# Reordering the tail of a two-layer transformer kernel: output merges, cluster logits and dense tiles on TensorE, copies and roots on ScalarE

## What is computed

```python
x = L0_attn_x
x = _layernorm(x + _L0_attn_ref(x, ...))   # 128 heads, latent projections
x = _layernorm(x + _L0_ffn_ref(x, ...))    # gated FFN with low-rank terms
x = _layernorm(x + _L1_attn_ref(x, ...))   # 32 heads, 8 key heads, causal
x = _layernorm(x + _L1_ffn_ref(x, ...))
```

```python
dots = jax.nn.softmax(x @ centroids.T / TEMPERATURE, axis=-1)   # 64 clusters
hits = dots > THRESHOLD
query_sel = jnp.any(hits, axis=1)        # one value a row
cluster_sel = jnp.any(hits, axis=0)      # one value a cluster, over all rows
row_sel = cluster_sel[assignments]       # one value an output column
dense = x @ weight.T + bias
out = jnp.where(query_sel[:, None] & row_sel[None, :], dense, 0)
```

## Time and profile before

| what | value |
|---|---|
| median of 3 runs | 2517.71 us (2509.7 to 2518.99) |
| the profiled execution | 2519.56 us, of which 2517.5 us are the span of the trace |
| PE busy in the span | 2465.6 us (98%) |
| DVE, ACT, POOL busy | 1555.6, 1396.0, 1152.8 us |
| granted TensorE clock, mean | 0.99 of full speed |
| first merge of the last key head starts | 2437.96 us into the span |

### The profile page before, as it was taken

The page is one execution under the profiler, slowest core; times in us unless marked ns, Lnnn a source line. Parts: engine busy times, 40 slices in busy tenths (PEclk is TensorE's granted clock), DMA queues, the critical chain, the costliest instruction groups (busy, mean ns, idle before and its releaser), DMA issues. The chain is left out here.

```text
span 2517.5 us, 40557 instructions
## 1 busy us (share of the span) xinstructions
PE 2465.6 (98%) x12632; PEld 1858.7 (74%) x12632; DVE 1555.6 (62%) x2796; ACT 1396.0 (55%) x2171; POOL 1152.8 (46%) x1155
## 2 busy tenths in 40 slices
PE   7999999999999999999998999899999999999998
PEld 4777777777777777777775588778888888888875
DVE  6666666666666666666664523276657557566576
ACT  3677777777777777777776433233424324234241
POOL 1556555555555555656564243234334234343331
PEclk9999999999999999999999999989999999999999
DMA  6122222222222222222221422121000010010100
GB/s 215 43 47 53 45 53 50 48 53 45 53 45 56 48 55 45 53 45 53 45 55 39 131 88 85 39 84 42 10 32 17 25 42 17 25 42 2 36 1 34
DMA packets 47613, 125.40 MB, mean 50 GB/s; under 512 B 6034, under 2 KB 23442, under 8 KB 41427
## 3 DMA queue, kind: packets, MB, share of 16 engines
q1 hardware_dynamic: 47570, 124.85, 18.5%
HBM read 80.27 MB, written 10.49 MB: 36 GB/s over the span
## 5 line engine op out<-in xcount | busy, mean ns | idle before, releaser
L427 DVE TENSOR_REDUCE row_max<-ps_max 128x1 f32<-128x512 f32 x1024 | 670.9, 688 | 193.0 <-PE ps_max L517 170.6
L292 POOL TENSOR_TENSOR p_parts<-probs,p_parts 128x1024 f16<-128x1024 f32 x256 | 547.5, 2149 | 367.0 <-ACT p_parts L346 366.0
L341 ACT ACTIVATE probs<-ps_score 128x1024 f32<-128x1024 f32 x512 | 523.1, 1022 | 241.8 <-PE ps_score L533 221.1
L531 PE MATMUL ps_score<-Q,K 128*128 128x512 f32 x1024 | 408.0, 398 | 2.2 <-ACT probs L341 2.1
L533 PE MATMUL ps_score<-Q,K 97*128 97x512 f32 x1024 | 407.1, 398 | 0.0
L517 PE MATMUL ps_max<-KX,Q 68*128 68x512 f32 x1024 | 378.8, 411 | 3.8 <-DVE row_max L427 3.6
L421 DVE TENSOR_TENSOR Q<-ps_x,Q 64x512 fp32r<-64x512 f32 x254 | 175.0, 689 | 241.9 <-ACT Q L336 238.2
L346 ACT ACTIVATE p_parts<-probs 128x1024 f16<-128x1024 f32 x256 | 269.5, 1053 | 4.0
L517 PEld LDWEIGHTS ps_max<-KX,Q 68*128 68x128 f32 x1024 | 189.3, 190 | 76.4 <-issue 28.1
L531 PEld LDWEIGHTS ps_score<-Q,K 128*128 128x128 f32 x1024 | 194.5, 190 | 60.4 <-ACT probs L341 12.0
L533 PEld LDWEIGHTS ps_score<-Q,K 97*128 97x128 f32 x1024 | 195.5, 191 | 39.3
(11 more groups left out here) (292 smaller groups left out, 4399.8 us busy)
## 6 DMA issues: line engine op xcount, KB each, us to landing
Q<-Q SPq DMA_DIRECT2D x64, 512.0 KB, 4.3
ffn_raw<-in_w_ffn SPq DMA_DIRECT2D x22, 768.0 KB, 4.4
w_raw<-in_w_qrope SPq DMA_DIRECT2D x32, 512.0 KB, 3.7
wq_raw<-in_wq SPq DMA_DIRECT2D x8, 1024.0 KB, 5.5
wo_raw<-in_wo SPq DMA_DIRECT2D x8, 1024.0 KB, 4.8
content_k<-probs SPq DMA_DIRECT2D x8, 512.0 KB, 6.8
Q<-content_q SPq DMA_DIRECT2D x64, 64.0 KB
K<-content_k SPq DMA_DIRECT2D x64, 64.0 KB
```

What stands on the lines that cost most here:

```text
L292: pool.tensor_tensor(p_lo[:, j, :, :], probs[:, j, 0:PAIRED, :], p_hi[:, j, :, :], ALU.subtract)\
L341: act.activation(probs[:, j, 2 * half:2 * half + 2, :], ps_score[half][:, :, :], ACT.Exp, scale=SCALE).then_inc(exped, 1)
L427: dve.tensor_reduce(row_max[:, t, j:j + 1], ps_max[t % 2][:, :], axis=AXX, op=ALU.max)\
L531: pe.matmul(ps_score[half][:, k, :], K1[:, b, t * P:(t + 1) * P], Q1[:, b, j, :], start=True, stop=False)
```

## The change

On PE the last merge moves in front of the first logits, with the transposes of tiles 6 and 7 behind these. Dense tile 0 now starts before the first logits are transposed, and the second logits, their transposes, the cluster count and the column's product stand two dense tiles earlier than before. On ACT each copy `high_x(t - 2)` stands in front of `root(t)`, and the copy of the first logits stands behind the load of the Exp table. DVE, POOL and SP keep their order. No instruction does other work than before; only the places at which dense tiles are cut differ.

```diff
--- before.py
+++ after.py
@@ -1577,11 +1577,10 @@
             take_outputs(KV, NU - 1)
             root(1, x_base)
             for t in range(2, TT):
+                high_x(t - 2)
                 root(t, x_base)
-                high_x(t - 2)
-                if t == TT - 2:
-                    take_logits(0)
             act.activation(unused[:, :], eps[:, :], ACT.Exp)
+            take_logits(0)
             high_x(TT - 2)
             high_x(TT - 1)
             exp_soft(0)
@@ -1961,37 +1960,34 @@
             merge(True, tk, 1)
             outputs(LAST, NU - 1)
             merge(True, tk, 2)
-            for t in range(TT - 3):
+            for t in range(ST + 1):
                 turn_x(t)
+                merge(True, tk, t + 3)
                 if t == 0:
-                    merge(True, tk, 3)
                     pe.wait_ge(o_low, ONE + LAST + 1)
-                    continue
-                if t == ST:
-                    pe.wait_ge(cl_ready, 1)
-                    logits(0)
-                merge(True, tk, t + 3)
-            turn_x(TT - 3)
+            turn_x(ST + 1)
+            pe.wait_ge(cl_ready, 1)
+            logits(0)
+            turn_x(TT - 2)
+            turn_x(TT - 1)
+            pe.wait_ge(cl_ready, 3)
+            dense_tile(0, 0, 6)
             turn_logits(0)
-            turn_x(TT - 2)
-            pe.wait_ge(cl_ready, 3)
-            dense_tile(0)
-            turn_x(TT - 1)
-            dense_tile(1)
+            dense_tile(0, 6)
             logits(1)
-            dense_tile(2, 0, 6)
+            dense_tile(1, 0, 4)
             turn_logits(1)
-            dense_tile(2, 6)
-            dense_tile(3)
+            dense_tile(1, 4)
+            dense_tile(2, 0, 4)
             for b in range(NB):
                 pe.wait_ge(hits, b + 1)
                 last = pe.matmul(ps_c[0:NCL, 0:1], any_hit[:, b, :], ones[:, 0:1], start=b == 0, stop=b == NB - 1)
             last.then_inc(hits_counted, 1)
-            dense_tile(4, 0, 6)
+            dense_tile(2, 4, 9)
             pe.wait_ge(onehot_made, 1)
             pe.matmul(ps_h[:, :], ones[0:NCL, :], onehot, start=True, stop=True).then_inc(column_made, 1)
-            dense_tile(4, 6)
-            for t in range(5, TT):
+            dense_tile(2, 9)
+            for t in range(3, TT):
                 dense_tile(t)
```

## The result

The changed kernel takes 2508.57 us (median of 22 runs, 2501.34 to 2514.8) against 2515.12 us (22 runs, 2509.62 to 2521.75) before. The ratio is 0.9972, with a 95% interval of 0.9964 to 0.9981. That is 0.28% or 7.0 us less, with an interval of 4.8 to 9.1 us (the two medians lie 6.55 us apart), where 6.9 was forecast. The interval leaves out 1, so it is a gain; the first three runs of before alone lay 9.3 us apart.

A forecast was written before the change was run, and what follows sets the result against it. PE, busy 98% of the span, and at the end DVE's queue behind a late column were the bound. 4.8 us from PE plus 2.1 from the queue made 6.9; 2517.71 - 6.9 = 2510.8, about 2511 us, range 2503 to 2516.

The forecast's parts named there:

- Copies in front of roots: On ACT: copies ahead of roots shrink DVE's round from 3.74 to about 2.81 us, with 0.58 us of cover.
- The ring that could have ended slower: Rival, chance 0.04: roots queue behind late copies, delaying PE, ACT and DVE over six tiles; time 2520.8 us.
- signs of being wrong: In the profile: PE waits for hits or onehot, roots start behind copies that waited, or the clock dips.
- Why `xl` was late: Ahead of the first logits: DVE idles 0.84 us each round for ACT's copy, which stands behind a root awaiting DVE.
- Merge 7 in front of the first logits: On PE: the 2.51 us wait ahead of the first logits goes, and 1.50 us of slow clock with it.
- Column and DVE's queue: At the end: masking begins at 2484.6 instead of 2496.14, tile 7 is masked at 2503.7 instead of 2510.61.
- PE's end: PE's last dense tile ends at 2503.5, 4.8 us before the earlier 2508.33.
- the queue: At the end: DVE no longer has a queue of tiles to mask, worth 2.1 us.
- The cover for the hits: At the count on PE: hits ready at 2480.9, PE there at about 2481.0; 0.1 us, uncertain by 0.5.
- Table load: On ACT behind the last root: the Exp table load costs nothing, with 1.7 us of cover.
- The total: Whole kernel: 4.8 us from PE and 2.1 from DVE's queue, 6.9 us less, about 2511 us.

The follow-up runs named there:

- a_copies_only: Kernel before with only ACT's copies put in front of its roots; masking of tile 7 at 57.13 us, ratio 0.9978.
- mc_roots_first: Changed kernel with ACT's roots in front of its copies again; masking of tile 7 at 61.78 us, ratio 0.9997.
- c_column_only: Kernel before with only second logits, count and column earlier on PE; masking of tile 7 at 61.81 us, ratio 0.9998.
- ma_late_column: Changed kernel with count and column back where they stood before; masking of tile 7 at 57.12 us, ratio 0.9977.
- ac_copies_column: c_column_only with ACT's copies also put in front of its roots; masking of tile 7 at 56.78 us, ratio 0.9976.
- h_count_early: Changed kernel with the cluster count nine matmuls earlier on PE; masking of tile 7 at 60.31 us, ratio 0.9997.
- f_bias_and_tail: Changed kernel with a shorter end on DVE and both bias parts in one product; last normalisation at 56.82 us, ratio 0.9953.
- b_one_bias: Changed kernel without the product of the bias's low part; masking of tile 7 at 53.21 us, ratio 0.9960.

## Why the prediction was right, point by point

- **Copies in front of roots.** Right, and worth more than its place in the sum suggests. DVE's round is 2.77 us (2.81 forecast), `xl` of tile 3 is ready 3.65 us before PE asks for it (3.7 forecast), and this part alone gives 5.01 us (a_copies_only). The ring that could have ended slower did not appear. One of the prediction's signs of being wrong did show, roots behind copies that themselves waited, but it was harmless: every root in the profile is released by DVE's moments, the closest one after 0.64 us of idleness (0.58 of cover forecast):

```profile
2463.60 0.60 ACT L1559 ACTIVATE xh<-ps_s 128x512 fp32r<-128x512 f32 x1 [1.41 <-PE ps_s L1921]
2464.84 0.29 ACT L1555 ACTIVATE dev<-moments,eps 128x1 f32<-128x1 f32 x1 [0.64 <-DVE moments L1682]
```

- **Why `xl` was late.** The prediction gave only the ring of DVE and ACT as the reason. The trace of before shows a second one, a start that was about 2 us late, told in the last section. That the exchange removes the whole wait does not depend on it.
- **Merge 7 in front of the first logits.** The wait of 2.51 us and the 1.50 of slow clock are gone, as forecast. But one sentence of this step misleads: "Even if the copies brought nothing, merge 7 alone (2.85) would cover the 2.51." It did cover that wait (mc_roots_first has none ahead of the first logits), and brought nothing by it (61.78 against the 61.81 of c_column_only): without the copies PE waited 3.08 us two steps later, for `turn_x(7)`. A merge set into the gap only postpones a wait for an engine whose own round (3.73 us) is longer than PE's (3.20); the engine stays as far behind as it was. With the copies moved, the wait ahead of the logits was gone without the merge (a_copies_only).
- **What the new order on PE is for.** The prediction gave it the wait ahead of the first logits. The runs give it another: it puts `turn_x(7)` early enough that the second logits need not wait for `xl` of tile 7 (1.41 us in ac_copies_column). I had not listed that wait, and so missed both kernels that have it.
- **Column and DVE's queue.** First masking step at 36.25 from the first `turn_x`, 36.13 forecast (2484.6 - 2448.47). With PE's end at 55.12 (55.03 forecast) and tile 7 at 55.16 (55.23), the 2.1 us for the queue were right: ma_late_column, which lacks only this, is 1.96 behind the changed kernel. The early column alone gives 0.33, and 0.35 on top of the copies, since it needs the other two.
- **The cover for the hits.** Forecast at 0.1 us, uncertain by 0.5 either way. In the profile the hits are finished at 2479.41 and the count starts at 2479.67, on time. By the prediction's own margin it was luck on which side of nothing this fell, and h_count_early shows what stood behind that narrow place.

```profile
2478.81 0.60 DVE L1727 TENSOR_REDUCE any_hit<-probs 128x64 f32<-128x256 f32 x1
```

```profile
2479.67 0.39 PE L1984 MATMUL ps_t<-ones_sb,any_hit 128*64 128x1 f32 x4
```

- **Table load.** ACT's copy of the logits ended at 2467.12 and PE asked for it at 2468.89: a cover of 1.8, 1.7 forecast. The instruction behind the load started 1.29 us after it. The 2.66 us with a drain that the Trainium skill gives in "ScalarE: Activation LUTs", section "What ACT_TABLE_LOAD costs", do not show here; the next ACTIVATE starts at once.
- **The total.** 6.9 forecast; 6.98 to the masking of tile 7 and 6.91 to the end of the span in the profile, 7.0 by the ratio. Both terms came out, 4.80 from PE's end (4.8 forecast) and 2.18 from the queue (2.1). The 2511 us leaned on a median of three runs that lay 2.6 us above the median of 22; from the latter it would have been 2508.2. The lower end of the range is a slip by its own terms: 2510 less 8.0 is 2502, not 2503.

## What to carry to other kernels

When an engine waits, look at the order on the engine that feeds it before filling the gap: a copy that was ready sat behind a root that was not, and exchanging the two brought 5.0 of 7.0 us. Parts that are worth next to nothing alone can be worth two microseconds together. On top of the copies PE's new order brings 0.01 us and the early column 0.35, and both together 1.97. So each reordering should be tried with the others in place as well as by itself. And a short wait on TensorE can cost more than its length: with a cover of 0.3 us or less on one side and a price of 5 us on the other, I would set the step one or two matmuls later; that was not run.

## What the runs showed of the hardware

- **The price of a short idle stretch on TensorE.** Behind 1.41 us of idle (ac_copies_column) the second logits' 12 matmuls ran at a granted clock of 1.00 and took 2.89 us (2473.68 to 2476.57). Behind 2.51 (before), 3.08 (mc_roots_first) and 2.00 us (h_count_early) the clock fell to its lower level. It cost 1.50 us in the first, about 1.5 in the second and 3.15 us in the last, the shortest of the three. The clock did not fall in the idle stretch itself, whose rows read 1.00, but behind it: in mc_roots_first PE worked at 1.00 from 2473.12 to 2474.50, and was at 0.50 from 2475.00 to 2477.50. Among these three the length of the idle stretch alone does not set the price; what does stays open here. Each is one execution; only the first was seen twice, in c_column_only with a wait of 2.52 us and 4.36 us for the logits.
- **DVE blocked by POOL.** In the changed kernel the first normalisation takes 4.73 us instead of 0.55, as it did before (4.72). It starts 0.12 us behind POOL's subtraction for the weight's low part, and ends 0.28 us behind that one's end:

```profile
2441.73 4.73 DVE L1695 TENSOR_SCALAR X<-X,moments,dev 128x512 f32<-128x512 f32 x1
```

```profile
2441.61 4.57 POOL L1492 TENSOR_TENSOR wq_lo<-wq_raw,wq_hi 128x2048 fp32r<-128x2048 f32 x1
```

  In f_bias_and_tail POOL's subtraction ran from 2447.43 to 2452.04; there the second normalisation was the long one, 2.50 us from 2449.82, again ending 0.28 behind POOL. The Trainium skill says in "SBUF — State Buffer", section "Who interferes with whom", that a `tensor_scalar` of DVE can run in a mode that needs the pair of ports shared with GpSimd, and that whoever issues first holds this pair for the whole instruction while the other is blocked. The trace agrees with the blocking; it does not show the mode. In the changed kernel it costs nothing, since `xl` is 3.65 us early all the same. In the kernel before it probably did cost something:

```profile
2443.22 4.72 DVE L1696 TENSOR_SCALAR X<-X,moments,dev 128x512 f32<-128x512 f32 x1
...
2450.63 0.68 DVE L1687 TENSOR_TENSOR X<-ps_r,X 128x512 f32<-128x512 f32 x1
```

  DVE works without a pause from the one row to the other, and takes up the sum of tile 2 at 2450.63, 2.16 us after merge 2 has ended (2448.47). A sum can start 0.2 behind its merge, so that by an estimate from these rows some 2 us of DVE's delay ahead of the first logits came from this block, and the slow round of 3.74 us kept it from catching up. No run takes POOL's subtraction away from the kernel before.
- **Runs differ by the clock.** The 22 runs of the changed kernel spread over 13.5 us, twice the gain. The fastest (2501.34) had a mean granted clock of 0.995, the slowest (2514.8) 0.988. In the profiled execution the clock is at 1.00 throughout the changed stage. Ahead of it the profiles differ although the code is the same: the first `turn_x` starts at 2438.91 us in h_count_early (mean clock 0.994) and at 2450.80 in b_one_bias (0.989). So most of the spread is likely to come from ahead of the stage. One of the 12 runs of h_count_early took 2536.49 us at a mean clock of 0.937; no trace of it is kept, and why stays open.
